# Transposing the halves of input and context by DMA instead of on TensorE, in a gated cross-attention block on one Trainium2 core

## The reference

```python
def _mha(query, key, value, Wq, bq, Wk, bk, Wv, bv, Wo, bo):
    q, k, v = proj(query, Wq, bq), proj(key, Wk, bk), proj(value, Wv, bv)
    scores = jnp.einsum('bhqd,bhkd->bhqk', q, k) / jnp.sqrt(dk)
    p = jax.nn.softmax(scores, axis=-1)
    x = jnp.einsum('bhqk,bhkd->bhqd', p, v)
    return jnp.einsum('bsd,ed->bse', merge_heads(x), Wo) + bo

x = x + tanh(g_xattn) * _mha(layernorm(x), ctx, ctx, Wq, bq, ...)
x = x + tanh(g_ffn) * ffn(layernorm(x), clip_x, clip_down, w_gate, w_up, w_down)
```

## Time and profile before

| | |
|---|---|
| median of 3 runs | 1910.21 us (1909.71 to 1914.14) |
| the profiled execution | 1910.74 us |
| its span, first to last instruction | 1909.0 us |
| TensorE busy | 88% of the span |
| VectorE | 76% |
| ScalarE | 45% |
| GpSimd | 26% |
| DMA queue of SP, share of 16 engines | 38.1% |

### The profile page before, as it was taken

The page is one execution under the profiler, slowest core; times in us unless marked ns, Lnnn a source line. Parts: engine busy times, 40 slices in busy tenths (PEclk is TensorE's granted clock), DMA queues, the critical chain, the costliest instruction groups (busy, mean ns, idle before and its releaser), DMA issues.

```text
span 1909.0 us, 36308 instructions
## 1 busy us (share of the span) xinstructions
PE 1687.6 (88%) x12892; PEld 832.0 (44%) x12892; DVE 1441.6 (76%) x1917; ACT 866.3 (45%) x1036; POOL 497.3 (26%) x686
## 2 busy tenths in 40 slices
PE   3788999989999899998999989986599999989787
PEld 3354444544445444454444444433344444434333
DVE  6648788787786877868778687777877778878555
ACT  2243433434335343353443533414777777756242
POOL 6123323223232232322323223212000000006634
PEclk6999999999999999999999999999799999999899
DMA  5233332323323233233332332225235454115897
GB/s 187 67 109 92 88 105 73 110 87 88 109 81 101 87 86 112 84 94 105 84 100 85 91 107 61 78 56 199 94 121 210 165 203 150 45 45 213 337 419 296
DMA packets 132189, 239.73 MB, mean 126 GB/s; under 512 B 17456, under 2 KB 66608, under 8 KB 129584
## 3 DMA queue, kind: packets, MB, share of 16 engines
q1 hardware_dynamic: 132144, 239.14, 38.1%
HBM read 126.10 MB, written 62.39 MB: 99 GB/s over the span
## 4 chain that ended last, share of the span: by engine, by line
issue 38%; PE 31%; DVE 16%; POOL 8%; DMA 5%; ACT 2%; POOLq 0%; DVEq 0%; SPq 0%; ACTq 0%
PE bank L1244 11%; PE bank L1149 5%; PE bank L1151 5%; PE bank L1150 5%; PE spair L1226 4%; DMA x<-out_dram 4%; DVE mx L842 3%; POOL xl L485 3%; DVE rs L834 3%; POOL yh L559 3%; DVE xbuf L806 2%; DVE v L826 1%; ACT xh L580 1%; DVE ndev L866 1%; DVE parts L821 1%
## 5 line engine op out<-in xcount | busy, mean ns | idle before, releaser
L593 ACT ACTIVATE pr<-spair 128x1024 f32<-128x1024 f32 x256 | 259.2, 1020 | 142.1 <-PE spair L1226 142.1
L842 DVE TENSOR_REDUCE mx<-spair 128x4 f32<-128x1024 f32 x256 | 304.4, 1212 | 0.0
L834 DVE RECIPROCAL rs<-bank 128x256 f32<-128x256 f32 x128 | 224.6, 1755 | 56.5 <-PE bank L1244 56.1
L821 DVE SCALAR_TENSOR_TENSOR parts<-bank,bqk,parts 128x512 f16<-128x512 f32 x128 | 94.5, 747 | 132.5 <-ACT parts L586 132.5
L515 POOL TENSOR_TENSOR ol<-o,oh 128x256 f16<-128x256 f32 x128 | 86.5, 675 | 389.7 <-ACT oh L602 380.8
L586 ACT ACTIVATE parts<-bank,bqk 128x512 f16<-128x512 f32 x128 | 88.0, 687 | 219.9 <-PE bank L1151 219.9
L1355 PE MATMUL spair<-xqT,wgT 128*128 128x512 bf16 x704 | 181.9, 381 | 1.2 <-ACT xqT L703 1.2
L1355 PE MATMUL spair<-xqT,wuT 128*128 128x512 bf16 x704 | 181.7, 381 | 0.0
L1244 PE MATMUL bank<-pr,v 128*32 128x256 f32 x2048 | 138.1, 387 | 27.2 <-DVE o L836 27.2
L1226 PE MATMUL spair<-stacks 128*128 128x256 f16 x1024 | 152.5, 275 | 6.5 <-DMA stacks<-mT 6.2
L686 ACT ACTIVATE sil<-spair,gsc 128x512 f32<-128x512 f32 x176 | 118.2, 680 | 74.9 <-PE spair L1355 74.9
(11 more groups left out here) (172 smaller groups left out, 3408.8 us busy)
## 6 DMA issues: line engine op xcount, KB each, us to landing
stacks<-parts SPq DMA_DIRECT2D x768, 64.0 KB, 2.0
x<-out_dram SPq DMA_DIRECT2D x32, 1024.0 KB, 11.0
h_spill<-hb SPq DMA_DIRECT2D x10, 2816.0 KB, 9.2
hb<-h_spill SPq DMA_DIRECT2D x10, 2816.0 KB, 15.6
xbuf<-in_x_dram SPq DMA_DIRECT2D x16, 1024.0 KB, 5.3
cbuf<-in_ctx_dram SPq DMA_DIRECT2D x16, 1024.0 KB, 5.3
xres<-in_x_dram SPq DMA_DIRECT2D x16, 1024.0 KB, 5.2
out_dram<-xres SPq DMA_DIRECT2D x16, 1024.0 KB, 4.3
```

Source lines behind the costliest of these rows:

```text
L593: act.activation(pr[:, u % 4, :, :, :].rearrange("p a b q -> p (a b q)"), spair[u % 2][:, :, :].rearrange("p a q -> p (a q)"), ACT.Exp, sc ...
L821: dve.scalar_tensor_tensor(out=parts[:, c, 2 * w + 1, :], in0=pj[g % 3][:, :], scalar=bqk[:, w, c:c + 1], in1=parts[:, c, 2 * w, :], op0=A ...
L834: dve.reciprocal(rs[:, g % 2, :], obank[:, S:2 * S]).then_inc(recip_done, 1)
L842: dve.tensor_reduce(mx[:, h:h + 2, b, :], spair[u % 2][:, :, :].rearrange("p a (q k) -> p a q k", q=KH), AX_X, ALU.max).then_inc(max_done, 1)
```

## The change

Four things change, all in the attention phase.

- The transposes go to the DMA engines. `turn`, `turns`, `turn_copy`, `turn_copies` and `prep_turns` are removed. SP issues eight transposing transfers for the context (`turn_c`) and eight for x (`turn_x`) per group, each of one half of one tile, 128 x 512 float16 (128 KB), straight from `ch`, `cl`, `xh`, `xl` to `cT` and `xT`. `turn_c(i + 1)` and `load_c(i + 2)` stand between the second and the third `stack`, `turn_x(i + 1)` and `load_x(i + 2)` behind the fourth; `mrow` now stands ahead of `store_x1`.
- `cT` has two buffers, so the loop bodies of SP and TensorE handle two groups per iteration.
- The halves are made tile by tile within the score steps: `high_c`/`high_x` on ScalarE and `low_c`/`low_x` on GpSimd, one tile a step (c in steps 0 to 3, x in steps 4 to 7). `x_tile_stats` are done in pairs in steps 0 and 1, with the moments in step 1; `x_norm_tile` stand in steps 3 to 6 and no longer in the tail. `x_rstds` follow the second `o_low`.
- The first three `qk` of a group wait for their banks by `x1_ready` of the previous group.

```diff
+            def turn_x(n):
+                wait(sp, qk_mm, n * 8, alone=True)
+                for t in range(NT):
+                    for s, (part, done) in enumerate(((xh, x_hi), (xl, x_lo))):
+                        wait(sp, done, n * NT + t + 1, alone=True)
+                        sp.dma_start_transpose(xT[:, :, s, t * P:t * P + P], part[:, t, :]).then_inc(xT_in, 16)
+            def turn_c(n, par):
+                wait(sp, qk_mm, n * 8 - 8, alone=True)
+                wait(sp, v_mm, n * NT - NT, alone=True)
+                for t in range(NT):
+                    for s, (part, done) in enumerate(((ch, c_hi), (cl, c_lo))):
+                        wait(sp, done, n * NT + t + 1, alone=True)
+                        sp.dma_start_transpose(cT[:, par, :, s, t * P:t * P + P], part[:, t, :]).then_inc(cT_in, 16)
...
+            turn_c(0, 0)
+            turn_x(0)
+            load_c(1)
             load_x(1)
-            load_c(1)
             for c in range(KC):
                 stack(0, None, c)
+            turn_c(1, 1)
+            turn_x(1)
+            load_c(2)
             load_x(2)
...
-            def body(i, j, nxt):
-                for c in range(KC):
-                    stack(i, j, c)
-                if nxt is not None:
-                    load_c(nxt)
-                    load_x(nxt)
+            def body(i, j, par, more):
+                stack(i, j, 0)
+                stack(i, j, 1)
+                if more > 0:
+                    turn_c(i + 1, 1 - par)
+                if more > 1:
+                    load_c(i + 2)
+                stack(i, j, 2)
+                stack(i, j, 3)
+                if more > 0:
+                    turn_x(i + 1)
+                if more > 1:
+                    load_x(i + 2)
+                mrow(i)
                 store_x1(j)
-                mrow(i)
                 load_res(j + 1)
...
+            def low_c(n, t):
+                wait(pool, c_hi, n * NT + t + 1)
+                wait(pool, cT_in, n * 128)
+                pool.tensor_tensor(cl[:, t, :], cbuf[:, t, :], ch[:, t, :], ALU.subtract).then_inc(c_lo, 1)
...
                 residual(j)
                 for g in range(NGR):
-                    o_low(j, g)
-                    if g == 3 and nxt is not None:
+                    if nxt is not None:
+                        if g < NT:
+                            low_c(nxt, g)
+                        else:
+                            low_x(nxt, g - NT)
+                    if g > 0:
+                        o_low(j, g - 1)
+                    if g == 2 and nxt is not None:
                         x_rstds(nxt)
...
+            def high_c(n, t):
+                if t == 0:
+                    wait(act, c_in, n * 16 + 16)
+                    wait(act, cT_in, n * 128)
+                act.activation(ch[:, t, :], cbuf[:, t, :], ACT.Copy).then_inc(c_hi, 1)
...
                     if nxt is not None:
-                        if g < NT:
-                            x_tile_stats(nxt, g)
-                        if g == NT - 1:
+                        if g < 2:
+                            x_tile_stats(nxt, 2 * g)
+                            x_tile_stats(nxt, 2 * g + 1)
+                        if g == 1:
                             x_moments(nxt)
+                        if g >= 3:
+                            x_norm_tile(nxt, g - 3)
...
                 if g == 0:
-                    wait(pe, xT_even, i * 4 + 4)
-                    wait(pe, xT_odd, i * 4 + 4)
+                    wait(pe, xT_in, i * 128 + 128)
+                    wait(pe, cT_in, i * 128 + 128)
                 if g >= 3:
                     wait(pe, qk_lo, i * 8 + g - 2)
+                elif before is not None:
+                    wait(pe, x1_ready, before * NT + (4, 2, 3)[g])
+                else:
+                    wait(pe, v_ready, (i - 1) * NT + (2, 3, 4)[g])
...
-                if nxt is not None:
-                    turns(nxt, range(TM), (x1_ready, j * NT + 2))
                 if i is not None:
                     turn_max(i)
-                if nxt is not None:
-                    turns(nxt, range(TM, 8), (x1_ready, j * NT + 2))
```

More of the change, by code:

```diff
@@ L527, in _ @@
             x_rstds(0)
-            low_parts(0)
-            pool.wait_ge(x_lo, 1)
+            for t in range(NT):
+                low_c(0, t)
+            for t in range(NT):
+                low_x(0, t)
+            pool.wait_ge(x_lo, NT)
             x_rstds(1)
-            low_parts(1)
+            for t in range(NT):
+                low_c(1, t)
+            for t in range(NT):
+                low_x(1, t)
             pool.wait_ge(const_done, 5)
@@ L888, in weight_int @@
                 dve.tensor_scalar(ffn_int[m], ffn_int[m], -QMAX - 1.0, None, ALU.max).then_inc(fw_int, 1)
-            def prep_turns(n, first):
-                for k in range(0, 8, 2):
-                    turn_copy(n, k, xT if k < 4 else cT, (first + k) % 3)
             weight_parts(0)
@@ L900, in _ @@
             weight_parts(3)
-            prep_turns(0, 1)
             for g in range(8):
@@ L1127, in _ @@
             pe.wait_ge(w_ready, 16)
-            def turn(n, k, bank):
-                src = (xh, xl) if k < 4 else (ch, cl)
-                if k == 0:
-                    wait(pe, x_hi, n + 1)
-                    wait(pe, x_lo, n + 1)
-                if k == 4:
-                    wait(pe, c_hi, n + 1)
-                    wait(pe, c_lo, n + 1)
-                kk = k % 4
-                dst = pj[bank][:, :].bitcast(F16)
-                for s in range(2):
-                    for t in range(NT):
-                        last = pe.transpose(dst[:, s * G + t * P:s * G + t * P + P],
-                                            src[s][:, t, kk * P:kk * P + P], id16[:, :])
-                last.then_inc(turned, 1)
             def three(dst, pairs):
@@ L1248, in pv @@
                 last.then_inc(pv_mm, 1)
-            def turns(n, ks, prev):
-                for k in ks:
-                    if k < 3:
-                        wait(pe, prev[0], prev[1] + k)
-                    else:
-                        wait(pe, (xT_even, xT_odd)[(k - 3) % 2], n * 4 + (k - 3) // 2 + 1)
-                    turn(n, k, (1 + k) % 3)
-            turns(0, range(8), (w_ready, 14))
             for g in range(8):
-                qk(0, g)
+                qk(0, g, 0)
                 if g >= 2:
@@ L1264, in _, with body @@
             for t in range(NT):
-                vproj(0, t)
+                vproj(0, t, 0)
                 if t < 2:
                     max_pair(0, 6 + t)
-            turns(1, range(8), (v_ready, 2))
             turn_max(0)
             pe.wait_ge(stack_ready, 2)
-            def body(i, j, nxt):
+            def body(i, j, par, before):
                 if i is not None:
-                    qk(i, 0)
+                    qk(i, 0, par, before)
                 score(j, 0)
```

119 lines of the change are left out of this document (52 added, 67 removed).

## The result

The changed kernel takes 1899.4 us in the median of 7 runs (1894.39 to 1903.89), the kernel before 1911.3 us in the same series (1909.71 to 1914.14). The ratio is 0.994, with a 95% interval of 0.9929 to 0.9952: faster by 12 us or 0.6%, where 78 us were predicted. The profiled execution of the changed kernel took 1898.31 us around a span of 1896.1 us.

A forecast was written before the change was run, and what follows sets the result against it. TensorE, 88% busy, was taken as the bound. Per period 6.56 - 0.8 - 0.05 = 5.7 us saved, over 14 periods 80 us, less 2.3 before the loop: 1910.2 - 78, say 1833 us; forecast's own range 1810 to 1850, overall 1808 to 2000.

The forecast's parts named there:

- (a): End of each group: without the transposes on TensorE, the next qk waits only for the last x1_tile, starting 4.56 us earlier.
- P: Time of one group's period in the attention loop, between two starts of qk(i, 0): 78.82 us before, predicted 73.1.
- (b): Tail of each group: four x_norm_tile leave VectorE's tail, regaining 2.0 us of waiting, with 0 and 3.0 as the ends.
- (c): Start of each group: VectorE's work formerly partly hidden behind the turns delays the first reciprocal and pv, costing 0.8 us.
- (d): Score steps: VectorE's extra statistic and moments in step 1, norm tiles in steps 3 to 6, are covered; cost 0 or 0.1 us.
- (e): Score steps: GpSimd's eight small subtractions between residual and o_low leave x_rstd 1.8 us of cover; cost taken as 0.
- Rival C: VectorE or ScalarE held up within the score steps, up to 1 us a step for four steps: 1890 us, chance 0.07.
- T: Time per transposing DMA, the longer of its SP issue and its passage through the DMA engines: taken as 1.28 us.
- The remainder of the chain: SP's transfer sequence per group besides 16 transposes: 47 us, so the next qk can't start before 47 + 16T.
- rivals A and B: Per-group transfers: A, they bound the kernel, T above 2.0, slower, chance 0.29; B, part of the gain, 1850 to 1925, 0.08.
- The estimate of T = 5.2: Transposing DMAs: by a skill page, four blocks without overlap would take 5.2 us, P = 131; the forecast did not adopt it.
- The prologue: Before the loop: first qk 3 us earlier, second at 109.8 us, 2.3 us later than before; net +2.3 us.

The follow-up runs named there:

- c2_halves_only: Kernel before with halves and norm tiles made in the score steps and GpSimd's order as changed, but transposes left on TensorE: 1927.5 us, ratio 1.009.
- e3_straight_and_order: Changed kernel with TensorE's loop written out straight and GpSimd's o_low ahead of the tile subtractions: 1849.5 us, ratio 0.9679.
- e1_straight_pe: Changed kernel with only TensorE's loop over pairs of groups written out straight, no jump back: 1893.5 us, ratio 0.9913.
- e5_three_mends: Changed kernel with TensorE's loop straight, o_low ahead of the tile subtractions, and another SP and GpSimd order ahead of the loop: 1838.9 us, ratio 0.9631.
- c1_before_double: Kernel before with only TensorE's loop changed to two groups per turn, no transposing transfers: 1933.7 us, ratio 1.0127.
- e9_double_turn_x: e5_three_mends with each transposing DMA of turn_x issued twice, the second into tiles that nothing reads: 1999.5 us, ratio 1.0458.
- e2_pool_order: Changed kernel with only GpSimd's o_low of a step moved ahead of that step's tile subtraction: 1878.4 us, ratio 0.9828.

## Why the prediction was wrong, step by step

The transposes left TensorE and its chain shortened as predicted, but the time did not follow: 12 us of 78, above the forecast's own range of 1810 to 1850. Two costs were missing from the sum: the waits behind GpSimd's subtractions, put at 0, and the fetches of a doubled loop body, for which there was no term. A third is the first period, which the sum took for one like the others.

- **(a) The turns go.** Right. But for the gaps, `qk` waits for `x1_tile` alone, and with the faults mended P is 73.6 us. The rearrangement without the DMAs, with the same fault in it, does not make the gain (c2_halves_only).
- **(b) Norm tiles out of the tail.** Right: the waits of `max_pair` for `mx` fall from 2.0 us to at most 0.42 us in a period.
- **(c) First wait of `pv`.** Right: 1.32 us, predicted 1.4.
- **(d) Covers in step 1 and steps 3 to 6.** By themselves they would have held: e3_straight_and_order has 0.28 us in step 7 and otherwise no wait there, except for 0.8 to 0.9 us in step 3 in two of 14 periods. What broke them was (e).
- **(e) GpSimd's small subtractions, "I take 0".** This step failed. I followed what `x_rstd` needs and found 1.8 us of cover; I did not ask who else waits for what is queued behind the subtractions. `o_low` is, and VectorE's `norm` two steps later waits for it. `x_rstd` itself came in time. The price at `pv` is 0.17 + 0.23 + 1.74 us per group (with the order mended only the last remains, at 0.28), the last of them with a stretch at half clock behind it in some groups. Mending it gives 21.0 us alone and 44.0 us on top of the straight loop. Rival C named the place ("GpSimd's small subtractions and the norm tiles get in each other's way") at P = 77 and a chance of 0.07. That P came to 77.29 is in part luck, for the fetches are in it; without them e1_straight_pe has 76.2 us.
- **TensorE's program was no term of the sum.** In the diff the loop body doubles, which I read as bookkeeping for `cT`. It is the smaller cost (6 us alone, 28.8 on top of the mended order), but nothing in the sum stood for it. Matmuls and weight loads alone counted, a period holds 641 matmuls and 642 weight loads before, 1,283 in a loop body. In the changed kernel it holds 577 and 578 (e5_three_mends' period above), 1,155, and the body of two groups 2,310; in c1_before_double it is 2,566. The first never shows a fetch in the loop, the other two stop at each jump back. The Trainium skill has the rule that I should have brought: "Runtime: NRT & Kernel Launch", section on instruction fetch mechanics, says that TensorE's store holds 2048 instructions and is refilled in blocks of 16 KiB, and that a taken branch whose target isn't in "the current 2-page window" forces a fetch before execution goes on. This case agrees on the stall and on the blocks (the packets of queue 8 are 16 KB each, 1.59 MB in 97). With the whole store as the window it agrees on the size too: 1,283 instructions loop without a fetch, 2,310 do not. Read as a window of two blocks, 512 instructions, the rule would have the kernel before fetch at every jump, and its trace shows no such packet from 200 to 1150 us; there the measurement decides.
- **The transfers.** T = 1.31 for 1.28, landing 2.5 us: right, and no transposing DMA was waited for in the loop. The remainder of the chain was mis-sized: 50.1 us in e5_three_mends and 83.7 - 31.4 = 52.3 in e9_double_turn_x instead of 47, so that `turn_x` is done at +71 and not by +66. The gain begins to shrink not at T = 1.63 but between (73.1 - 52.3) / 16 = 1.30 and (73.1 - 50.1) / 16 = 1.44. The forecast stood closer to rivals A and B than I had written; that the transfers just fitted is in part luck.
- **The estimate of T = 5.2.** By "VectorE: DVE Perf Modes" in the Trainium skill, section on the three transpose paths, four blocks one after the other would have given it. Here one of 128 KB is issued each 1.31 us and landed after 2.5, less than the 5.2 of the estimate; so for this size the blocks overlap, and the measurement decides.
- **The prologue.** `qk(1, 0)` at 108.57, predicted 109.8: right. But I stopped the sum there. Behind the last transpose on SP stand two 1 MB loads and then `mrow`, and the first `score` behind `qk(1, 0)` waits another 4.04 us for that. The first period is 84.68 us instead of 73.1, which is 11.6 of the 66 us. It falls to 80.05 with the first two mends and to 77.60 with SP's order, which also brings `qk(1, 0)` from 110.20 to 104.45; together the new order gives 10.7 us in the median.
- **Two ends of ranges.** By its own terms the forecast's lower end is 1910.2 - 14 x (4.56 + 3.0 - 0.05) - 7 = 1798 us and not 1810, and rival B's upper end, at T = 2.0, is some 1938 and not 1925. The result lies in neither difference.

The budget closes: 66 us of miss, of which e3_straight_and_order returns 49.9 and e5_three_mends another 10.7. The 5.9 left are, in e5_three_mends, 14 x 0.5 = 7 us for P of 73.6 instead of 73.1 and 4.0 us more in its first period (77.6), less 5.4 for `qk(1, 0)` at 104.45 instead of 109.8. How the 49.9 us divide between the fetch and GpSimd's order can't be said as two numbers, since the mends are not additive; each way round, the order is the larger.

## What to carry to other kernels

When work moves between engines, list for every instruction that is put into a queue what stands behind it there and who waits for that, to the end of the chain; `o_low` was found neither by busy shares nor by the cover of its own consumer. Count the instructions in a hardware loop's body before you double it, and look whether the instruction queue moves anything in the loop: if it does only with the doubled body, write the loop out straight. Keeping the body at one group, by indexing the buffer with a register, is another way that was not tried here. And judge a rearrangement with its small faults mended one by one and together: apart they gave 6, 21 and 7 us, together 60.5, and the same DMAs with one more order of VectorE and SP gave 92.

## What the runs showed of the hardware

- The jump back to a body of 2,310 or 2,566 matmuls and weight loads left TensorE idle for 3.35 to 3.91 us, where it otherwise waited 1.2 to 1.6 us for another engine, and for 4.07 to 7.16 us in e2_pool_order, where 1 MB transfers ran. A body of 1,283 fetched nothing. A straight program of the same instructions fetched as well (57 packets of 16 KB from 200 to 1150 us in e1_straight_pe) and never waited.
- After such a gap, and after the 22.59 us wait in the prologue, the granted clock is at the lower of its two levels, 1.2 GHz of 2.4: matmuls of 0.38 us take 0.60 to 0.63, for about 2.5 us in the loop (from 502.85 to 505.38).
- A transposing DMA from SBUF to SBUF with 128 KB costs SP 1.19 to 1.27 us of issue in most rows, about twice that of a 64 KB stack copy (0.64 to 0.71), and one follows another each 1.31 us. So 16 of them per period take 21 us of SP, and the DMA engines' share rose from 0.32 to 0.47 (200 to 1150 us).
- A transfer of 16 KB that SP issued right behind 1 MB loads landed 9.0 us after its issue (`mrow`, 108.53 to 117.5), against 2.3 us in the median of the loop.
